# Second attention: GpSimd may send four transfers a step, not two, in the last batch

## What is computed

```python
x = x + attn_a(layernorm(x), ...)                 # encoder block
x = x + ffn(layernorm(x), ...)                    # experts, stage "m" of the kernel
x = x + attn_b(layernorm(x), Wq, Wk, Wv, Wo, bo)  # causal attention, 16 heads of 8, stage "b"
x = x + ffn(layernorm(x), ...)                    # experts, stage "n"

def ffn(x):
    probs = sigmoid(x @ router_w.T + expert_bias)
    top_w, top_idx = top_k(probs, 8)              # 8 of 160 experts for each token
    combine = ...                                 # top_w normalised, times 2.5
    h1w = silu(einsum('th,eih->eti', x, w_gate)) * combine.T[:, :, None]
    return einsum('eti,ehi->th', h1w, w_down) + shared(x)
```

## Time and profile before

| what | us |
|---|---|
| median of 3 runs | 2441.11 (2428.94 to 2441.45) |
| the profiled execution | 2439.89 |
| its span, first to last instruction | 2437.4 |
| around the span | 2.49 |
| stage "b" ends, stage "n" starts | 1935.9 and 1937.8 |
| first gather of stage "n" | 2096.8 |

### The profile page before, as it was taken

How to read it: one execution, slowest core, us unless ns; L and a number is a source line. 1 busy time by engine, 2 the same in 40 slices (tenths; PEclk the granted TensorE clock), 3 DMA queues, 4 the chain that set the end, 5 groups by cost and what they waited for, 6 DMA issues and landing times. The chain is left out here.

```text
span 2437.4 us, 44931 instructions
## 1 busy us (share of the span) xinstructions
PE 1800.4 (74%) x15531; PEld 1040.3 (43%) x15531; DVE 1645.0 (67%) x4636; ACT 1139.9 (47%) x2101; POOL 1274.5 (52%) x1244
## 2 busy tenths in 40 slices
PE   8997786787687678873979888988898878783000
PEld 4555454454445455551334443434343356562000
DVE  8477587587677664576888878887888266375222
ACT  4663553554454355661447554544454546663000
POOL 0162166667657674773336530441252477577776
PEclk9998798799799688995789977888898879997555
DMA  9940101201203687874223220203121378785222
GB/s 360 344 191 30 44 4 59 76 6 44 79 20 149 234 276 231 269 250 119 50 80 85 57 79 21 68 32 86 36 81 46 133 289 285 243 275 163 60 60 56
DMA packets 143464, 309.19 MB, mean 127 GB/s; under 512 B 30668, under 2 KB 45644, under 8 KB 137340
## 3 DMA queue, kind: packets, MB, share of 16 engines
q1 hardware_dynamic: 110472, 239.16, 29.6%
q0 software_dynamic: 32768, 67.17, 9.4%
HBM read 163.12 MB, written 142.70 MB: 125 GB/s over the span
## 5 line engine op out<-in xcount | busy, mean ns | idle before, releaser
L1537 POOL DMA_INDIRECT slots_in<-g_xs,g_place x512 | 517.4, 1011 | 297.4 <-ACT b_pT L2628 146.3
L2628 ACT ACTIVATE b_pT<-b_psE 128x512 f32<-128x512 f32 (+3 forms) x768 | 332.1, 492 | 379.4 <-PE b_psE L2529 201.1
L1564 POOL DMA_INDIRECT r_xs<-slots_out,g_place x336 | 329.3, 980 | 231.4 <-issue 86.6
L2380 DVE TENSOR_REDUCE b_peak<-b_psM 128x1 f32<-128x512 f32 (+3 forms) x768 | 388.8, 551 | 80.1 <-PE b_psM L2512 48.8
L2509 PE MATMUL b_psM<-b_stacks 72*128 72x512 bf16 (+3 forms) x768 | 262.5, 380 | 55.8 <-DVE b_peak L2380 23.2
L2525 PE MATMUL b_psE<-b_stacks 75*128 75x512 bf16 (+3 forms) x768 | 238.4, 365 | 14.5 <-ACT b_pT L2628 12.7
L1564 POOL DMA_INDIRECT g_xs<-slots_out,g_place x176 | 173.7, 987 | 92.6 <-issue 50.3
L2539 PE MATMUL b_psV<-b_pT,b_vb 128*32 128x512 f32 (+3 forms) x1536 | 180.8, 553 | 4.4 <-ACT b_ctxu L2635 4.1
L2509 PEld LDWEIGHTS b_psM<-b_stacks 72*128 72x128 bf16 x768 | 79.9, 106 | 226.1 <-DVE b_peak L2380 135.9
L2145 DVE COPY m_staged_w<-wgd 128x192 f32 x512 | 107.8, 280 | 89.4 <-PE m_psY L1850 81.2
L2145 DVE COPY n_staged_w<-wgd 128x192 f32 x512 | 106.7, 278 | 83.6 <-PE n_psY L1850 75.9
(11 more groups left out here) (658 smaller groups left out, 3987.3 us busy)
## 6 DMA issues: line engine op xcount, KB each, us to landing
wgd<-in_w_gdT SPq DMA_DIRECT2D x20, 1536.0 KB, 9.3
slots_in<-g_xs SPq DMA_DIRECT2D x26, 1024.0 KB
m_rows<-slots_in SPq DMA_DIRECT2D x104, 256.0 KB
slots_out<-m_y SPq DMA_DIRECT2D x104, 256.0 KB
n_rows<-slots_in SPq DMA_DIRECT2D x104, 256.0 KB
slots_out<-n_y SPq DMA_DIRECT2D x104, 256.0 KB
key_dash<-a_dashes SPq DMA_DIRECT2D x32, 512.0 KB, 6.2
a__arg<-key_dash SPq DMA_DIRECT2D x32, 512.0 KB
```

Of the source, the lines that this page charges most:

```text
L1537: self.nc.gpsimd.indirect_dma_start(self.G.slots_in[self.h], bass.IndirectOffsetOnAxis(self.G.place[:, TPH * self.h + t, k:k + 1], 0), sel ...
L1564: self.nc.gpsimd.indirect_dma_start(self.rows(i)[:, k, :], None, self.G.slots_out[t // TPH], bass.IndirectOffsetOnAxis(self.G.place[:, t, ...
L2380: nc.vector.reduce_max(to, taking()[:, 0:size], AX.X).then_inc(m_taken, 1)
L2628: nc.scalar.activation(pT[:, e % KEPT, h, q0:HALF], psE[:, j % BANKS, q0:HALF], ACT.Exp, scale=SCALE).then_inc(e_taken, 1)
```

## The change

One number becomes two: in steps of the last batch (`step < LAST * GB * NS` is false, that is from step 144 on) `transfers` may issue four, in all other steps two as before.

```diff
-SEND_A_STEP = 2
+SEND_A_STEP, SEND_A_LAST_STEP = 2, 4
...
             def transfers(step):
 
-                left = SEND_A_STEP if step < BATCH * GB * NS - DRAINED_STEPS else 0
+                left = (SEND_A_STEP if step < LAST * GB * NS else SEND_A_LAST_STEP) if step < BATCH * GB * NS - DRAINED_STEPS else 0
                 asked = min(left, TOPK * gather.tiles - gather.asked)
```

## The result

| | us |
|---|---|
| before | 2441.11 (2428.94 to 2444.29, 7 runs) |
| after | 2464.3 (2447.91 to 2466.14, 7 runs) |
| ratio | 1.0082, 95% interval 1.0061 to 1.0104 |

By the ratio that is 20 us more, between 15 and 25; the two medians are 23.2 us apart. The prediction had 2453.0, 11.9 us above the median of before, with a range up to 2460.

A forecast was written before the change was run, and what follows sets the result against it. No engine is busy throughout; VectorE closes the attention, and GpSimd would end 14.1 us behind it. Sum: 2439.89 + 14.1 (late transfers) + 0.3 (exit) - 1.3 (relief in stage "n") = 2453.0 us, range 2443 to 2460.

The forecast's parts named there:

- The third batch's transfers: End of the attention: 48 transfers in 60.9 us from 1889.16, ending at 1950.0, 14.1 us behind VectorE.
- I take +0.3 for six semaphore waits: Exit from the attention after GpSimd's last transfer: its queue is free at once, so only 0.3 us is added.
- The bound above: Upper limit for the attention's exit: 2.2 us more if it waited for the last transfer's landing.
- Ahead of the third batch, nothing: Attention from step 144: last `values` copy 7.6 us later under some 115 us of cover, so no cost.
- I take zero: Second batch's steps: denser transfers don't slow VectorE, whose 128x480 operation takes 658 ns with or without transfers.
- The relief in stage "n", -1.3: Stage "n": six removed transfers no longer precede the load on the chain, 6 x 0.224 = 1.3 us gained.
- the 2.4 us named: Sign of being wrong: first gather nearer to stage "n"'s start than the earlier 159.0 us by more than 2.4.
- The rival by which the relief pays the delay back: Stage "n": earlier loads and a higher TensorE clock give back up to 5.4 us, 2448.9; relief above 3 us 0.10.
- TensorE starts colder: Rival, start of stage "n": lower clock after longer idling costs 5.5 us, 2458.5; chance 0.12 together with the longer wait.
- The port rule: VectorE and GpSimd lock one port pair; transfers would gain beside an idle VectorE at the layer's end; no gain taken.
- the step 174: ScalarE's step in the attention that releases the third batch's first transfer at 1889.16; its moving would be a sign of error.
- If GpSimd idles at the barrier: Sign of being wrong at the attention's end: the changed profile was to show no GpSimd idleness there.

## Why the prediction was wrong

- **The third batch's transfers: right.** 48 transfers took 60.8 us (60.9 predicted), and their last ended 14.94 us behind VectorE (14.1 predicted). The 0.8 is the first transfer's lead over VectorE's end: 1935.89 - 1889.16 = 46.7 in the profile of before, 45.9 in the one of after.
- **The failed step: the way out after a GpSimd transfer, "I take +0.3 for six semaphore waits", and with it "GpSimd has 1935.89 - 1919.82 = 16.1 us to spare".** The reason given was "The engine's queue is free at once after a transfer in all rows", which holds for the next transfer and not for the stage's last instruction. The exit cost 9.22 us in a DRAIN, and the slack of before was none: its DRAIN ended 0.34 us after VectorE. The row that showed this stood in the trace of before and was not asked for, because the rows of busy instructions show only the idle time and "POOLq L100" as its end. With it the sum would have been 2439.89 + 14.1 + 9.2 + 0.3 - 0.3 - 1.3 = 2461.9; it is worked out here afterwards, and the 9.2 in it needs the price for each transfer, which the DRAINs of before would have given (5.31 us after 64).
- **The bound above was wrong in kind.** "if the exit waited for landing, 2.2 us more" priced the wait that I could think of. The DRAIN starts up to 57 us after the last transfer's end and costs the same.
- **Ahead of the third batch, nothing: not quite.** The kernel that makes only this part of the change is at 1.0001 (0.9977 to 1.0025), so no large cost is there. But from the second batch's first transfer to VectorE's end every profile with denser transfers has at least 1.3 us more. The rows behind "I take zero" were three instructions of one kind on VectorE, and they don't show how long a step takes.
- **The relief in stage "n", -1.3: not shown, nor refuted.** The two profiles of the changed kernel have -0.73 and +0.61, and leaving out the same 24 transfers moved the time by -3 (+1 to -7). The first gather stood 158.3 us after the start of the stage, within the 2.4 us named. The rival by which the relief pays the delay back is out: the delay stands in the time nearly whole.
- **TensorE starts colder: no.** It stood still for 29.6 us over the boundary and not 5.32, took 1.12 us for its first two transposes and 0.66 for the third (1957.71), where in the trace of before the fourth (1952.17) was the first with 0.66; the granted clock over the 158 us is 0.87 in both.
- **The port rule** of the Trainium skill, "SBUF — State Buffer", section "SBUF: two separate sides": no run here shows transfers that gain by standing beside an idle VectorE. They kept their 0.97 us and 0.30 between them on both sides of its end.
- **What the changed profile would show:** the step 174 held, and the gap up to the places was 25.59 us (25 predicted). "If GpSimd idles at the barrier" was named as a sign of being wrong, and it is where the error sat: 11.14 us.

In sum: +14.94 + 9.22 - 0.34 + 0.32 - 0.73 + 0.17 = +23.6 us where +13.1 was predicted; of the 10.5 us between them the DRAIN is 8.9. The 1.3 us ahead of VectorE's end come on top, +24.9 in all, beside 23.2 between the medians.

No version beat the kernel before. The nearest with more of the third batch's transfers in the attention, three per step with a DRAIN in the idle stretch, is at 1.0015.

## What to carry to other kernels

An engine's slack at a barrier ends with its queue, not with its last busy row: ask the trace for DRAIN and other sequencer instructions at the stage's end, on every engine, before counting idle time as slack. Work that is issued ahead from an engine's idle time may leave a debt that grows with the count, to be paid where all engines wait; if the amount can't be lowered, pay it earlier, in an idle stretch of that engine that nothing follows at once. And where a row shows that a queue is free for the next instruction of one kind, it says nothing of the next of another.

## What the runs showed of the hardware that was not expected

- A DRAIN of GpSimd's queue takes 0.082 to 0.084 us for each indirect transfer of 128 rows still counted, between 24 and 112 of them, whether the last ended 0, 7 or 57 us before; 64 transfers in the first attention took 5.31. Fewer fit less well: after 18, in the trace of before, it took 2.05 us behind the last transfer's end (0.114 each), after 6 it took 0.58 (0.097). Over its last 7 us in the changed kernel the DMA engines carry nothing.
- 160 gathers leave only 48 to be counted, and the 288 transfers up to the second batch's last leave 64.
- Executions of one kernel differ by 15 us and more here (2447.91 and 2466.14 of the changed one; 2438.93 and 2472.72 of the one with the added DRAIN), and the start of stage "b" alone by 5.7 between the two profiles; the stretch between two marks repeats far better (26.09 and 26.21 for the boundary in the two profiles of the changed kernel).
- The granted clock of one stretch of the attention was between 0.83 and 0.91 in the profiles, and the stretch took 197.1 and 187.4 us.
